# Loading the slot weights of layer 0 one stage earlier, into a weight buffer that is free there

## The reference, cut to what matters

```
x = x + L0_attn(layernorm(x))
x = x + L0_xattn(layernorm(x), ctx, ctx)        # 16 heads of 8 features
x = x + L0_ffn(layernorm(x))                    # mixture of 64 experts with 32 slots each
x = x + L1_attn(layernorm(x)) ...
```

## Time and profile before

| what | value |
|---|---|
| median of 3 runs | 3878.59 us (3874.23 to 3881.83) |
| the profiled execution, its own time | 3872.76 us |
| its span in the profile | 3870.8 us |
| instructions | 90218 |
| cross attention of layer 0 in the span | about 253 to 542.8 us |
| fold block | 542.8 to 558.1 us |
| dispatch of layer 0 | 558.1 to about 838 us |
| granted TensorE clock, mean | 0.967 |

### The profile page before, as it was taken

How to read it: one execution, slowest core, us unless ns; L and a number is a source line. 1 busy time by engine, 2 the same in 40 slices (tenths; PEclk the granted TensorE clock), 3 DMA queues, 4 the chain that set the end, 5 groups by cost and what they waited for, 6 DMA issues and landing times. The chain is left out here.

```text
span 3870.8 us, 90218 instructions
## 1 busy us (share of the span) xinstructions
PE 3487.4 (90%) x30145; PEld 2573.1 (66%) x30145; DVE 2694.2 (70%) x5859; ACT 2435.9 (63%) x9586; POOL 2059.7 (53%) x2590
## 2 busy tenths in 40 slices
PE   8989979988989989999898998899899997788797
PEld 5656645557877868888665664666688873456587
DVE  6867749977765757777687886644577753879822
ACT  6959944445543437777544991455688866579655
POOL 4534329968983424434265540275666634456744
PEclk9999999999999989999999999999999999899988
DMA  8013410010000000000000003135500004200078
GB/s 109 2 25 48 55 34 1 1 55 1 1 1 35 2 8 6 6 6 6 5 2 8 12 8 118 28 99 88 218 22 22 21 28 133 93 5 10 30 258 303
DMA packets 320104, 185.18 MB, mean 48 GB/s; under 512 B 214104, under 2 KB 289127, under 8 KB 318613
## 3 DMA queue, kind: packets, MB, share of 16 engines
q1 hardware_dynamic: 304294, 148.02, 14.1%
q0 software_dynamic: 13568, 27.36, 3.0%
q10 hardware_dynamic: 1792, 4.04, 0.3%
HBM read 131.43 MB, written 50.54 MB: 47 GB/s over the span
## 5 line engine op out<-in xcount | busy, mean ns | idle before, releaser
L3673 POOL DMA_INDIRECT l2f_b_xb<-l2f_tokens,l2f_inv x160 | 155.6, 973 | 172.5 <-issue 157.8
L2663 POOL TENSOR_TENSOR l1x_Sx<-l1x_Sx,l1x_sm 128x512 f32<-128x512 f32 x128 | 132.2, 1043 | 188.5 <-DVE l1x_sm L2859 188.5
L2663 POOL TENSOR_TENSOR l3a_Sx<-l3a_Sx,l3a_sm 128x512 f32<-128x512 f32 x128 | 133.5, 1044 | 128.9 <-DVE l3a_sm L2859 127.3
L1389 PEld LDWEIGHTS l0f_acc<-l0f_d_xk,l0f_d_Z 128*128 128x128 f32 x1024 | 124.7, 191 | 113.8 <-POOL l0f_d_Z L1357 112.8
L2963 ACT ACTIVATE l1x_Sx<-l1x_Sx,l1x_nmx 128x128 f32<-128x128 f32 x512 | 199.1, 393 | 1.7 <-DVE l1x_nmx L2853 1.7
L2963 ACT ACTIVATE l3a_Sx<-l3a_Sx,l3a_nmx 128x128 f32<-128x128 f32 x512 | 198.9, 392 | 0.0
L835 ACT ACTIVATE l3f_Pr<-l3f_S,l3f_nmx 128x128 f32<-128x128 f32 x512 | 182.5, 402 | 3.4 <-DVE l3f_nmx L763 3.4
L835 ACT ACTIVATE l2x_Pr<-l2x_S,l2x_nmx 128x128 f32<-128x128 f32 x512 | 184.0, 426 | 0.7 <-DVE l2x_nmx L763 0.7
L835 ACT ACTIVATE l0a_Pr<-l0a_S,l0a_nmx 128x128 f32<-128x128 f32 x512 | 182.6, 406 | 0.7 <-DVE l0a_nmx L763 0.7
L1273 ACT ACTIVATE l0x_Pr<-l0x_S,l0x_nmx 128x128 f32<-128x128 f32 x512 | 181.5, 404 | 1.9 <-DVE l0x_nmx L1190 1.7
L1389 PE MATMUL l0f_acc<-l0f_d_xk,l0f_d_Z 128*128 128x128 f32 x1024 | 144.5, 284 | 25.1 <-POOL l0f_d_Z L1357 24.9
(11 more groups left out here) (773 smaller groups left out, 11944.9 us busy)
## 6 DMA issues: line engine op xcount, KB each, us to landing
l3f_b_W<-in_l3f_we SPq DMA_DIRECT2D x72, 514.0 KB, 5.2
l3f_sorted<-l3a_blank SPq DMA_DIRECT2D x1, 17680.0 KB, 51.2
l3x_Mb<-l3x_dram_max SPq DMA_DIRECT2D x32, 512.0 KB, 4.2
l2f_results<-l2f_b_ys SPq DMA_DIRECT2D x40, 256.0 KB, 2.4
l2f_W<-in_l2f_w SPq DMA_DIRECT2D x1, 6144.0 KB
l3f_b_xb<-l3f_sorted SPq DMA_DIRECT2D x72, 65.0 KB, 4.2
l0f_ew<-in_l0f_ew SPq DMA_DIRECT2D x1, 4096.0 KB
l3f_XS<-l3f_results SPq DMA_DIRECT2D x8, 512.0 KB, 6.6
```

What stands on the lines that cost most here:

```text
L1389: mm = nc.tensor.matmul(acc[q][:, k * P:(k + 1) * P], quarter(b, q)[:, k * P:(k + 1) * P], xk[:, b % 2, :], start=False, stop=False, skip_ ...
L2663: pool.tensor_tensor(quad(Sx, s, q), quad(Sx, s, q), bcast_in(sm[:, s, 4 * q:4 * q + 4], P), ALU.mult).then_inc(w_done, 1)
L3673: pool.indirect_dma_start(xb[:, j % 16, :], None, rows[:, :], bass.IndirectOffsetOnAxis(inv[:, j:j + 1], 0), bounds_check=None).then_inc(x ...
```

## The change

The three loads of `fold_bias` are issued by SP during the cross attention, at the start of its turn t = 4, ahead of `back(1)`. They go into `C.big`: its first half takes `phi`, its second half `phi_last`. Two of the loads cover 127 rows and not 128, so that row 127 of `phi` can be loaded with `phi_b` at once; row 127 of `phi_last` is set to zero beforehand by a memset of the whole half on POOL (before its step 4), which SP waits for (`phi_clear`). One subtraction over all 128 rows then leaves the bias row as it is. `fold_bias` loses SP's list, the wait of PE and two of the four `hold_clock` matmuls; its DVE list waits for the three loads, 48 on `C.phi_in`. `phiX` and `last` are no longer allocated.

```diff
+def phi_halves(C):
+    return [C.big[:, 2 * n:2 * n + 2, :].rearrange("p n c -> p (n c)") for n in range(2)]
...
 def stage_l0_xattn(nc, C, sems, d, X):
...
+        phi, phi_last = phi_halves(C)
...
+                def load_phi():
+                    sp.wait_ge(phi_clear, 1)
+                    sp.dma_start(phi[0:P - 1, :], d["l0f_phiT"][0:P - 1]).then_inc(C.phi_in, 16)
+                    sp.dma_start(phi[P - 1:P, :], d["l0f_phi_b"].rearrange("(a n) -> a n", a=1)).then_inc(C.phi_in, 16)
+                    sp.dma_start(phi_last[0:P - 1, :], d["l0f_phiT"][P - 1:P].to_broadcast([P - 1, SLOTS])).then_inc(C.phi_in, 16)
...
                 for t in range(GROUPS + 3):
+                    if t == 4:
+                        load_phi()
                     if 0 <= t - 3 < GROUPS:
                         back(t - 3)
...
                 for b in range(-AH - 1, NB):
+                    if b == 4:
+                        pool.memset(phi_last[:, :], 0.0).then_inc(phi_clear, 1)
                     step(b)
...
 def fold_bias(nc, C, sems, d, phiX, last, XT, zero, acc):
...
-            pe.wait_ge(phi_in, 32)
-            hold_clock(nc, C, idle, 4)
-
-        @block.sync
-        def _(sp):
-            sp.dma_start(phiX[:, :], d["l0f_phiT"]).then_inc(phi_in, 16)
-            sp.dma_start(last[:, :], d["l0f_phiT"][P - 1:P].to_broadcast([P, SLOTS])).then_inc(phi_in, 16)
-            sp.wait_ge(minus_done, 1)
-            sp.dma_start(phiX[P - 1:P, :], d["l0f_phi_b"].rearrange("(a n) -> a n", a=1)).then_inc(row_in, 16)
-            sp.wait_ge(row_in, 16)
+            hold_clock(nc, C, idle, 2)
...
-            dve.wait_ge(phi_in, 32)
+            dve.wait_ge(C.phi_in, 48)
             nc.vector.tensor_tensor(phiX[:, :], phiX[:, :], last[:, :], ALU.subtract).then_inc(minus_done, 1)
...
 def stage_l0_ffn(nc, C, sems, d, X):
...
-        phiX = sb("phiX", [P, SLOTS])
+        phiX, last = phi_halves(C)
...
-            last = sy("last", [P, SLOTS])
```

More of the change, by code:

```diff
@@ L978, in stage_l0_attn @@
                        wo=w[:, 3, :], out_bias=bo[:, :], beside=beside)
+SLOTS = 2048
+def phi_halves(C):
+    return [C.big[:, 2 * n:2 * n + 2, :].rearrange("p n c -> p (n c)") for n in range(2)]
 def stage_l0_xattn(nc, C, sems, d, X):
@@ L1013, in stage_l0_xattn @@
          s_mm, max_done, exp_done, tp_mm, pt_done, r_done, n_mm, out_done, on_done, o_moved, o_in0, o_in1, ht_done,
-         x_done, biased, early_done) = sems(29)
+         x_done, biased, early_done, phi_clear) = sems(30)
         qp_in, kv_in, o_in = [qp_in0, qp_in1], [kv_in0, kv_in1], [o_in0, o_in1]
@@ L1314, in stage_l0_xattn @@
         sems.clear()
-SLOTS = 2048
 EXPERTS, PER = 64, 32
@@ L1479, in fold_bias @@
 def fold_bias(nc, C, sems, d, phiX, last, XT, zero, acc):
-    phi_in, row_in, minus_done, zero_done = sems(4)
+    minus_done, zero_done = sems(2)
     with nc.psum_tensor("l0f_idle", [P, 512], F32) as idle, nc.Block() as block:
@@ L4297, in build @@
         C.v_stored = ctx.enter_context(nc.semaphore("l0x_v_stored"))
+        C.phi_in = ctx.enter_context(nc.semaphore("phi_in"))
         C.x_out = ctx.enter_context(nc.semaphore("x_out"))
```

## The result

| | before | changed |
|---|---|---|
| median | 3878.15 us (4 runs) | 3942.41 us (4 runs, 3938.4 to 3949.16) |
| ratio | | 1.0174, 95% interval 1.0162 to 1.0187 |
| profiled execution, span | 3872.76, 3870.8 us | 3938.40, 3936.5 us |

The account below looks back on a forecast made before the run. TensorE, busy 90% of the span, was taken to bound the kernel, with stages in sequence. Terms -8.9 - 0.85 + 64.6 + 2.5 = +57.4 us put it at 3936 us against the median, range 3893 to 3968.

Parts of the forecast that it names:

- (a): Fold block: with loads landed before and two hold_clock matmuls fewer, the next block starts at 549.2, not 558.1: -8.9 us.
- (b): Start of the dispatch: if PE's clock holds, DVE gets its first bank two passes earlier: -0.85 us, bounds 0 and -1.7.
- (c): POOL's memset of phi_last before step 4 takes 1.76 us of its idle time: cost 0, bounds 0 and +1.8.
- (d): SP's wait for phi_clear comes after queries(3), which need POOL's work three steps behind the memset: cost 0.
- (e): SP's queue: 127-row loads run on one DMA engine, 79 us against 5 us spread; issuing them costs 0.
- the sign that the heads would be issued some 80 us after the strips: SP's queue in cross attention: heads' issue follows back(1)'s strips by some 80 us, not 8.
- (f): Cross attention, step 12: PE waits for the heads of group 1, queued behind the loads and back(1)'s strips: +64.6 us.
- (g): Behind that stall: queries(4) land late for step 14 and PE restarts at half rate: +2.5 us, bounds 0 and 6.
- The sum: Whole kernel: -8.9 - 0.85 + 64.6 + 2.5 = +57.4 us, giving 3936 against the median.
- Rival B: SP's queue: loads spread over 16 engines in unequal shares, stage loses 0 (to +3): 3869 us; chance 0.15.
- Rival C: SP's queue: each load on one engine, but different ones; stall 25.1 us, +17.9 in all, 3896 us; chance 0.05.

Follow-up runs that it names:

- experiment 1: The changed kernel with each 127-row load cut into 112 and 15 rows: median 3871.96 us, ratio 0.9987.
- experiment 2: The changed kernel with only the load of phi cut into 112 and 15 rows, the broadcast left at 127: 3902.18 us, one execution.
- experiment 3: The changed kernel with each 127-row load cut into 122 and 5 rows: 3905.11 us, one execution.
- experiment 4: The changed kernel with the three loads, uncut, issued by POOL in its own queue before its step 8: 3871.23 us, one execution.
- experiment 7: The changed kernel with loads cut into 112 and 15 rows, issued later, at SP's turn t = 8 behind queries(7): median 3870.71 us, ratio 0.9986.
- experiment 9: The same kernel as experiment 7, measured a second time: median 3869.58 us, ratio 0.9977.
- experiment 10: The changed kernel with the three loads, uncut, issued by POOL in its own queue before its step 26: median 3864.34 us, ratio 0.9972.
- experiment 6: The kernel before with POOL's 128x2048 memset put into the cross attention three times, nothing loaded there: 3866.49 us, one execution.
- experiment 8: The kernel of experiment 7 without the two hold_clock matmuls of the fold block: median 3871.41 us, ratio 0.9986.

## Why the prediction was right, point by point

- **(a) The fold block**, -8.9: measured -8.86, with PE's passes ending it at 623.54 (621.66 + 1.88) as computed. The new block took 6.25 or 6.26 us in all eight profiles that have it; the old one scattered (12.62 to 15.85), so the gain lies between 6.4 and 9.6. DVE's subtraction and POOL's memset ran side by side in 2.23 and 3.51 us and were not in each other's way.
- **(b) The start of the dispatch**, -0.85 with bounds to -1.7: POOL's first subtraction came 6.23 us behind the block instead of 7.57, -1.34. The whole dispatch took 279.0 to 279.1 us in experiments 1 to 4, 7 and 9, 1.3 less than before, but 280.41 in the profile of the changed kernel, where it was lost again later in the stage (why isn't shown), and 280.87 in experiment 10, where the clock fell. Nor is the gain the change's alone: in experiment 6 the old block was followed by passes at full rate and a dispatch of 279.02 us. The first passes were at full rate in seven of eight profiles with the new block, and in one of four with the loads in the block.
- **(c), (d) Memset and `phi_clear`**, 0: right; experiment 6 shows the first by itself.
- **(e) One engine for 127 rows**: right, and now counted in packets for 127, 122, 112, 15 and 5 rows. The rate was right too: in 385 to 430 us 1124 - 977 = 147 rows went over in 45 us, 0.306 us each, for 0.31. Wrong in this step was that SP's issue costs 0. I reckoned 1.1 us for three issues; they took 20.2, and the next strips 65. SP did not lay transfers for a busy engine into the queue without limit; it stopped. Most of this cost nothing, because the wait for `o_moved` stood behind it anyway: the same time, shown as issue and not as a wait. So the sign that the heads would be issued some 80 us after the strips did not come as written: the strips began late, and it was 67.7.
- **(f) The stall**, +64.6: 66.9 measured, 2.3 us more, and closer than its steps, which miss both ways. Counted from step 12, which came 3.9 us later in this profile, the rows began 2.3 us later than reckoned (362.7 in the trace), and took 78.0 us, not 79. The strips then needed 5.7 us and not 3.7 (440.7 to 446.3), with five of them issued only from 440.88 on. And the 1.8 us from the last data to the semaphore was a misreading of the earlier trace rows: behind 549.4 its slices still show single rows of 8 KB (36 GB/s), the last of which started at 550.66, and its small packet came at 550.96, 0.3 us ahead of DVE. Here SP issued the heads 0.7 us behind the last strip's data.
- **(g) What is late next**, +2.5: 3.81 measured, and the reason was half right. queries(4) were not late: their strips were out by 460.5, and the transposes of q at 464.90 have no wait. What was late is the clock: after 67 us of idle PE works at half rate until 461, 2.08 us for four score passes at 450.89 that took 1.13, and the step lasts 12.43 us (450.06 to 462.49) instead of 7.17. That is +5.3, near the upper bound of 6; in experiments 2 and 3, after 31 and 26 us of idle, it is +5.9. The 3.81 is smaller because a late step that took 8.75 us in the kernel before, with passes at half rate, took 7.17 here, by chance.
- **The sum**, +57.4, against +65.7 between the two profiles (+64.3 between the medians). The difference of 8.3: +2.3 from (f), +1.3 from (g), +0.9 from (b), and +3.9 (5.33 - 1.45) in stretches ahead of the change's first instruction, where the clock fell otherwise by chance. The rest is below 0.1.
- **Rival B** (spread loads, -9.75 and 0 to +3 for the queue) was wrong of this kernel, but experiments 1, 7, 9 and 10 make it true. Their ratios, 0.9987, 0.9986, 0.9977 and 0.9972, are -5 to -11 us where it said -9.75. The intervals of 9 and 10 hold that value, that of 1 touches it (0.9975), that of 7 (from 0.9977) just misses it. Part of the shortfall can be that the old fold block is at times shorter than the 15.11 I started from, and its first logits at times fast; a cost of a few us elsewhere for the versions on SP's queue can't be excluded by these runs.
- **Rival C** (two different engines) would have given a wait of 25 us; it was 66.9.

## What to carry to other kernels

Before moving a load into a queue that others need, count how many DMA engines its outermost size can be divided over: in SP's queue 127 rows ran on one engine, 122 on two, 112 on 16. Cutting 127 rows into a multiple of 16 and a rest cost one more issue of some 0.5 us for each load, and was worth 70 us for the two. The packet counts of an earlier profile show the number of engines, since each transfer counted here added one small packet per engine used.

## What the runs showed of the hardware

- SP stopped in the middle of issuing with a load of 127 rows (39 us) ahead on one engine: the next issues took 3.26, 16.47, 38.47 and 19.54 us, where 0.3 to 0.8 was usual. Such a queue shows as long issues, not as waits.
- POOL's queue dealt the same 127 rows out over the engines (65 small packets for three loads, 9.9 us to landing); a DMA issue there took 0.54 to 0.82 us of POOL (experiments 4 and 10).
- TensorE's clock after the fold block: with twelve passes at full rate and 2.26 us of idle behind them, the first logits ran at full rate (1.98 us for four passes) in seven of eight profiles and at half (3.78) in one; with eight passes and the same idle, at half (3.66) in the one profile of experiment 8. After 67, 31, 26 and 4.3 us of idle in the middle of the cross attention PE went on at half rate for 8.6 to 13 us.
